# A four-layer Fourier tower in one launch: image pairs 0 and 31 stay in SBUF from layer to layer, two weight buffers in place of three, and seven eighths of mixing's chunk 0 loaded within the forward stage

## The chip, the cores and the metric

The kernel is one launch on one core of one Trainium2 chip. The metric is the device time of that launch in microseconds (us), the median of the runs shown. Five engines work from their own instruction streams and meet at semaphores: TensorE (PE, with its weight loads as PEld), VectorE (DVE), ScalarE (ACT), GpSimd (POOL) and SyncE (SP). SP does no arithmetic here; its queue issues the loads from DRAM and the stores of spectra. ACT's queue issues the stores of the layers' results besides its own work. SBUF is seen as 128 partitions; PSUM as eight banks of 128 x 512 float32.

## What is computed

A tower of four layers over 64 images of 64 x 64 pixels and 64 channels, followed by a head and a small transformer tail. All of it is float32. The layer loop, cut from the reference:

```python
for l in range(LAYERS):                                   # 4
    xf = jnp.fft.rfft2(h)                                 # only 32 x 16 modes are used
    of[:, :, :M1, :M2]  = einsum('bixy,ioxy->boxy', xf[:, :, :M1, :M2],  w1[l])
    of[:, :, -M1:, :M2] = einsum('bixy,ioxy->boxy', xf[:, :, -M1:, :M2], w2[l])
    sc = jnp.fft.irfft2(of)
    pw = einsum('bihw,oi->bohw', h, pw_w[l]) + pw_b[l]
    y = sc + pw
    y = (y - y.mean((0, 2, 3))) * rsqrt(y.var((0, 2, 3)) + EPS) * gamma[l] + beta[l]
    h = gelu(y)
out = gelu(h @ fc1_w + fc1_b) @ fc2_w + fc2_b
```

The mean and the variance go over all images, so `gelu(y)` of a layer can't be applied before the last image's `y` is there. That puts a barrier at the end of each layer.

## The kernel before, in words

The 64 images are 32 pairs (`NP`); a pair fills 128 partitions (two images x 64 channels) with 4,096 values each (`PX`), 2 MiB (2.10 MB). A layer is three stages, with all engines meeting after each (`phase_end`, L165 to L173):

- **Mixing** (`*_mix`): eight chunks (`NCH`) of the spectrum. A chunk needs its spectra of all images (`spec_in[c]`, 2 MiB, L382), its weights (`w_modes[l, c]`, 2 MiB, L375), a negated copy of the imaginary half by ACT (L460) and a copy of the real half by DVE (L471). PE multiplies (L444), DVE turns the result (L482), SP stores it in four pieces (`spec_out`, L391, 4 x 512 KiB). Three buffers for the weights, three for the spectra. After chunk c is multiplied SP loads spectra and weights of chunk c + 3, then waits for the turned result and stores it. At the end it loads the first input pair (L531) and the first group of mixed spectra (L517) ahead.
- **Inverse** (`*_inverse`): for each pair PE does the inverse transform (L581, L604) and the pointwise product with the pair's input (L595); ACT adds the bias and copies PSUM to SBUF (`y_out`, L661, four pieces T = 0 to 3), and stores the pair with two DMAs (L667); DVE turns (L697) and takes moments (L705). From layer 1 on the input pair is the stored `y` of the layer before: SP loads it (L531, three buffers `hin`), ACT applies norm and GELU in place (L653, two halves). `yout` has two buffers, so ACT's copy of pair p waits until pair p - 2 is stored. After the last pair ACT waits for both stores' semaphores, then computes the square root (L682) between DVE's L740 and L742.
- **Forward** (`*_forward`, after layers 0 to 2): SP loads `y` again (L773, four buffers `hf`, two pairs already at the end of the inverse stage, L563), ACT applies GELU (L843), DVE turns (L848, L853, L862), PE transforms (L805, L822), SP stores the spectrum of each group of four pairs (L778). The weights of the next layer's chunks 0 to 2 are loaded near its end; after the last group's store has landed, mixing begins.

Layer 0 takes the image `x` with three channels as input, so its mixing is fed by a spectrum computed at the start, and its inverse stage has no GELU. After layer 3 the head reads `y` once more (L905). The order within an engine is the order in which the code is written; nothing is rescheduled. SP's waits hold everything behind them on its queue.

Of the kernel before, what the change touches and what calls it, by code (L numbers as in the profile page):

```python
# [13 lines left out]
P = 128  # L14
C = 64
S = 64
PX = S * S
# [85 lines left out]
def build(nc, d, B, out):  # L103
# [5 lines left out]
    with ExitStack() as ctx:  # L109
# [246 lines left out]
        w_loaded = [sem(f"w_loaded{u}") for u in range(3)]  # L356
# [7 lines left out]
        w_sb = [at(u * MC * C, MC, C) for u in range(3)]  # L364
        s_sb = [at(3 * MC * C + 2 * u * B * MC, 2, B, MC) for u in range(3)]
        m_sb = [at(3 * MC * C + 6 * B * MC + 2 * u * B * HB, NG, 2, GI * HB) for u in range(2)]
        ROW = (slice(0, C), slice(C, P))
        USES = [len(range(u, NCH, 3)) for u in range(3)]

        def third(l, c):  # L370

            return l * (USES[c % 3] * 16) + (c // 3 * 16 + 16)

        def load_weights(sp, l, c):
            sp.dma_start(w_sb[c % 3], d["w_modes"][l, c]).then_inc(w_loaded[c % 3], 16)  # L375

        def sync_mix(sp, l, first):
            def load(c):
# [3 lines left out]
                sp.dma_start(s_sb[u][:, 0], spec_in[c]).then_inc(s_loaded[u], 16)  # L382
                if c > 2 or first and c == 2:
                    load_weights(sp, l, c)
# [40 lines left out]
        def tensor_mix(pe, l, first):  # L425
            for c in range(NCH):
                u, n = c % 3, l * NCH + c
                pe.wait_ge(w_loaded[u], third(l, c))
                pe.wait_ge(real_down, n + 1)
                for v in range(2):  # L430
# [3 lines left out]
                    for turn in range(4):  # L434
# [4 lines left out]
                        for k in range(4):  # L439
                            for half in range(2):  # L440
                                for row in range(2):
# [3 lines left out]
                                                   w_sb[u][ROW[row], mode, :], s_sb[u][ROW[row], :, :, mode],  # L445
# [6 lines left out]
        def scalar_mix(act, l, first):  # L452
# [3 lines left out]
            for c in range(NCH):  # L456
                u = c % 3
                act.wait_ge(s_loaded[u], third(l, c))
                for v in range(2):
                    act.activation(s_sb[u][0:C, 1, :, v * K1:(v + 1) * K1], s_sb[u][C:P, 0, :, v * K1:(v + 1) * K1],  # L460
                                   ACT.Copy, scale=-1.0).then_inc(imag_up, 1)

        def vector_mix(dve, l, first):
# [3 lines left out]
            def rotate(c):  # L467
                u = c % 3
                dve.wait_ge(s_loaded[u], third(l, c))
                dve.sem_inc(waited[dve.engine], 1)  # L470
                dve.tensor_copy(s_sb[u][C:P, 1], s_sb[u][0:C, 0]).then_inc(real_down, 1)  # L471
# [30 lines left out]
        grp = [at(off, M2, GI, HB) for off in (8 * PX, PX)]  # L502
        yout = [at((3 + u) * PX, PX) for u in range(2)]
# [3 lines left out]
        IN_USES = [len(range(b, NP, 3)) for b in range(3)]  # L507
# [25 lines left out]
        def sync_inverse(sp, l, first):  # L533
            if first:
# [3 lines left out]
                for b in range(3):  # L538
                    sp.sem_inc(in_loaded[b], IN_USES[b] * 16)
# [11 lines left out]
            for p in range(NP):  # L551
                if first:
                    load_x(p)
                elif p > 0:
# [7 lines left out]
            for q in range(2):  # L562
# [1529 lines left out]
```

## Time and profile before

| | |
|---|---|
| median of 3 runs | 4284.08 us (4277.56 to 4299.02) |
| profiled execution | 4291.21 us, its span 4289.4 us |
| PE / DVE / ACT busy | 75% / 56% / 49% of the span |
| DMA moved | 1119.64 MB, 261 GB/s over the span |
| mixing / inverse / forward of one layer (layer 1; forward ahead of it) | 137 / 418 / 287 us |
| head and tail, after the tower | about 1080 us |

The time of a stage is read from the timeline: forward 623 to 910 us, mixing 917 to 1047 us with its last store landing until 1060, inverse 1060 to 1465, then normalization until 1488. The layer pattern repeats with little change. Rows with "SPq" or "ACTq" are DMA issues on those queues; "landing" is from an issue to the completion of its bytes; what stands in brackets after a timeline row is the idle time of the engine ahead of it and who ended it.

### The profile page before, as it was taken

The page shows a single profiled execution, that of the slowest core. Times are in us where ns is not written, and L with a number is a line of the kernel's source. Part 1 is how long each engine was busy: PE and PEld are TensorE (multiplying, and loading weights), DVE is VectorE, ACT ScalarE, POOL GpSimd, SP SyncE. Part 2 cuts the span into 40 slices and gives each one's busy share as a digit, 9 for nine tenths or more (in the row PEclk, how much of TensorE's full clock was granted, in tenths as well). Part 3 has the DMA queues.
Part 4 walks back from the last instruction along what each step waited for, and adds up shares of the span by engine and source line. Part 5 has one row for each costly group of instructions (what it writes and reads, how often), then busy time and mean ns, then how long its engine had stood idle before and what let it go on. Part 6 is the DMA issues. An engine that isn't in the chain of part 4 may idle for free. (4 is left out here: it accounts for less than half of the span.)

```text
span 4289.4 us, 122178 instructions
## 1 busy us (share of the span) xinstructions
PE 3236.5 (75%) x54724; PEld 2080.3 (48%) x54724; DVE 2394.2 (56%) x3232; ACT 2090.2 (49%) x1756; POOL 28.9 (1%) x48
## 2 busy tenths in 40 slices
PE   5968866667888566687876666878869996759777
PEld 4746644456555344575554444755542221743532
DVE  3456669963666589645655996456540001454556
ACT  2123345521666555216765553166659996222322
POOL 0000000000000000000000000000000001000000
PEclk8989988888999889899998898999989998669688
DMA  8979887879999877799998786999985441012053
GB/s 314 349 196 248 226 266 276 300 287 356 364 383 374 307 284 297 272 354 364 391 379 310 290 310 269 357 358 385 387 318 207 179 165 66 1 28 53 1 106 64
DMA packets 181647, 1119.64 MB, mean 261 GB/s; under 512 B 25561, under 2 KB 31905, under 8 KB 107326
## 3 DMA queue, kind: packets, MB, share of 16 engines
q1 hardware_dynamic: 140988, 843.27, 54.3%
q10 hardware_dynamic: 39234, 269.45, 18.1%
q8 instruction: 316, 5.18, 0.5%
q0 software_dynamic: 1024, 1.05, 0.1%
q14 instruction: 85, 0.70, 0.0%
HBM read 708.56 MB, written 405.14 MB: 260 GB/s over the span
## 5 line engine op out<-in xcount | busy, mean ns | idle before, releaser
L604 PEld LDWEIGHTS bank<-fb,arena 64*64 64x64 f32 x16384 | 670.0, 199 | 521.8 <-issue 507.7
L604 PE MATMUL bank<-fb,arena 64*64 64x128 f32 x16384 | 675.4, 294 | 244.8 <-ACT arena L661 196.2
L661 ACT ACTIVATE arena<-bank,pwb 128x1024 f32<-128x1024 f32 x512 | 559.1, 1111 | 475.7 <-PE bank L595 351.3
L705 DVE BATCH_NORM_STATS2 stats<-arena 128x6 f32<-128x512 f32 x1024 | 629.0, 676 | 191.1 <-ACT arena L661 190.8
L595 PE MATMUL bank<-arena,wst 64*64 64x512 f32 x4096 | 625.6, 635 | 12.9 <-issue 12.8
L843 ACT ACTIVATE arena<-arena,shift,scale 128x1024 f32<-128x1024 f32 x384 | 443.7, 1229 | 324.9 <-DMA arena<-y_dram 324.7
L697 DVE STREAM_TRANSPOSE arena<-bank 128x512 f32<-128x512 f32 x512 | 321.1, 684 | 454.2 <-PE bank L581 454.2
L653 ACT ACTIVATE arena<-arena,shift,scale 128x2048 f32<-128x2048 f32 x192 | 401.5, 2093 | 320.0 <-issue 206.1
L805 PE MATMUL bank<-arena,fwq 32*32 32x512 f32 x6144 | 285.2, 746 | 333.6 <-DVE arena L848 333.6
L444 PE MATMUL bank<-arena 64*64 64x128 f32 x8192 | 453.9, 393 | 103.4 <-DVE arena L471 83.6
L444 PEld LDWEIGHTS bank<-arena 64*64 64x64 f32 x8192 | 397.5, 154 | 159.5 <-issue 112.2
L848 DVE STREAM_TRANSPOSE arena<-arena 128x1024 f32<-128x1024 f32 x384 | 440.0, 1203 | 16.4 <-ACT arena L843 16.4
L581 PE MATMUL bank<-arena,ga 64*64 64x512 f32 x2048 | 301.8, 613 | 90.2 <-DMA arena<-spec_out 72.6
L822 PE MATMUL bank<-arena,ghq 32*32 32x256 f32 x12288 | 351.4, 425 | 12.1 <-issue 7.6
L460 ACT ACTIVATE arena<-arena 64x2048 f32<-64x2048 f32 x64 | 118.8, 1903 | 432.9 <-DMA arena<-spec_in 432.9
L822 PEld LDWEIGHTS bank<-arena,ghq 32*32 32x32 f32 x12288 | 281.5, 111 | 86.3 <-issue 53.3
L805 PEld LDWEIGHTS bank<-arena,fwq 32*32 32x32 f32 x6144 | 96.2, 112 | 440.9 <-issue 429.1
L482 DVE STREAM_TRANSPOSE arena<-bank 128x512 f32<-128x512 f32 x256 | 159.7, 683 | 247.3 <-PE bank L444 131.3
L919 PE MATMUL bank<-arena,fc 64*128 64x512 f32 x1024 | 264.1, 624 | 18.8 <-ACT arena L947 17.4
L954 ACT ACTIVATE arena<-bank,fc1b 128x1024 f32<-128x1024 f32 x256 | 267.7, 1123 | 13.5 <-PE bank L919 13.5
L853 DVE STREAM_TRANSPOSE arena<-bank 128x1024 f32<-128x1024 f32 x192 | 226.7, 1218 | 21.2 <-PE bank L805 20.5
L972 DVE TENSOR_SCALAR arena<-bank,fc2b 128x512 f32<-128x512 f32 x8 | 6.0, 751 | 398.0 <-PE bank L930 398.0
(195 smaller groups left out, 2475.9 us busy)
## 6 DMA issues: line engine op xcount, KB each, us to landing
arena<-y_dram SPq DMA_DIRECT2D x224, 2048.0 KB, 10.3
y_dram<-arena ACTq DMA_DIRECT2D x256, 1024.0 KB, 13.4
arena<-in_w_modes SPq DMA_DIRECT2D x32, 2048.0 KB, 17.5
arena<-spec_in SPq DMA_DIRECT2D x32, 2048.0 KB, 14.6
spec_out<-arena SPq DMA_DIRECT2D x128, 512.0 KB, 14.8
arena<-spec_out SPq DMA_DIRECT2D x116, 512.0 KB, 16.5
spec_in<-arena SPq DMA_DIRECT2D x24, 2048.0 KB, 13.6
spec_in<-arena SPq DMA_DIRECT2D x4, 4096.0 KB, 12.0
```

Of the source, the lines that this page charges most:

```text
L444: mm = pe.matmul(bank[4 * v + q][ROW[half], k * 2 * B:(k + 1) * 2 * B], w_sb[u][ROW[row], mode, :], s_sb[u][ROW[row], :, :, mode], start=( ...
L581: mm = pe.matmul(bank[2 * v + r][CHAN[par], :], ga[k_p, r * S:(r + 1) * S], grp[p // Q % 2][k_p, :, par * Q + q, :], start=True, stop=True ...
L595: mm = pe.matmul(bank[4 + T % 2 * 2 + i][CHAN[v], :], wst[CHAN[i], :], hin[p % 3][CHAN[i], px:px + BK], start=False, stop=True, tile_posit ...
L604: mm = pe.matmul(hpx(bank[4 + T % 2 * 2 + i][CHAN[v], :])[:, :, j * S:(j + 1) * S], a2[p % 2][CHAN[i], v, :, 4 * T + j], hpx(fb2[CHAN[i], :]),
L653: act.activation(x, x, ACT.Gelu, bias=shift[:], scale=scale[:]).then_inc(h_ready, 1)
L661: act.activation(hpx(yout[u])[:, :, T * BK:(T + 1) * BK], banks[:, 4 + T % 2 * 2:6 + T % 2 * 2, :], ACT.Identity, bias=pwb[:]).then_inc(y_ ...
L697: dve.transpose(a2[p % 2][:, :, v * HB + c0:v * HB + c0 + 16, :].rearrange("p v c r -> p c v r"), banks[:, 2 * v:2 * v + 2, :].rearrange(" ...
L705: dve.bn_stats(stats[:, p * 48 + 6 * t:p * 48 + 6 * t + 6], hpx(yout[p % 2])[:, i, T * BK:(T + 1) * BK]).then_inc(y_seen, 1)
L805: mm = pe.matmul(bank[g][QUAD[c], :], fwq[QUAD[g], s * 32:(s + 1) * 32], hT[q % 2][QUAD[g], s, :, c * CQ:(c + 1) * CQ], start=(s == 0), st ...
L822: mm = pe.matmul(bank[4 + c][QUAD[j], 0:256], ghq[QUAD[c], col:col + K1], t1[q % 2][QUAD[c], v:4:2, hh, :, ri * M2:(ri + 1) * M2], start=( ...
L843: act.activation(x, x, ACT.Gelu, bias=shift[:], scale=scale[:]).then_inc(f_ready, 1)
L848: dve.transpose(hT[p % 2][:, :, 16 * v:16 * v + 16, :].rearrange("p s h c -> p h s c"), hf[p % Q][:, v * 2 * BK:(v + 1) * 2 * BK].rearrang ...
```

## The change

Two pieces of 4,096 values per partition at the top of the arena, `kept[0]` and `kept[31]`, hold pairs 0 and 31 from the inverse stage of one layer to that of the next. For them `y_out` writes straight into `kept` (it was one activation of 128 x 1024 a piece, and is four of 64 x 512, since the layout that the store's DMA used to make is now made by the copy), nothing is stored, the forward stage and the head apply GELU in place and don't load, and the next inverse stage finds them with GELU already applied, so it neither loads them nor applies it. `FED` is the list of the other 30 pairs; counts of semaphores follow it.

The room comes from mixing: two weight buffers (`NW = 2`), and five pieces for the spectra where there were six: real halves in three, second planes in two (`planes`), so that ACT's and DVE's plane copies of chunk c wait for chunk c - 2's product. With two buffers the weights of chunk c + 2 are loaded after the product of chunk c, ahead of the spectra of chunk c + 3; only chunks 0 and 1 are loaded within the forward stage. In the freed place there the spectra of images 0 to 55 of chunk 0 are loaded too, after the stores of the groups 0 to 6; the last eight images follow at mixing's start.

```diff
+        NW = 2
+        KEPT = (0, 31,)
+        kept = {p: at(ARENA - (i + 1) * PX, PX) for i, p in enumerate(KEPT)}
+        FED = [p for p in range(NP) if p not in KEPT]
...
-        w_sb = [at(u * MC * C, MC, C) for u in range(3)]
-        s_sb = [at(3 * MC * C + 2 * u * B * MC, 2, B, MC) for u in range(3)]
+        w_sb = [at(u * MC * C, MC, C) for u in range(NW)]
+        s_all = at(NW * MC * C, 5, B, MC)
...
+        EARLY = B - GI
+        def load_spectra(sp, c, images):
+            sp.dma_start(s_all[:, c % 3, images], spec_in[c][:, images]).then_inc(s_loaded[c % 3], 16)
+        def planes(c):
+            first, second = c % 3, 3 + c % 2
+            return s_all[:, first:second + 1:second - first]
...
             for c in range(NCH):
+                if NW == 2 and c + 2 < NCH:
+                    sp.wait_ge(mix_done, (l * NCH + c) * 2 + 2)
+                    load_weights(sp, l, c + 2)
                 if c + 3 < NCH:
                     load(c + 3)
                 store(c)
                 if c == NCH - 3:
-                    if not first:
+                    if not first and 0 not in KEPT:
                         load_input(sp, l, 0)
...
                 act.wait_ge(s_loaded[c % 3], spectra_count(l, c))
+                if c > 1:
+                    act.wait_ge(mix_done, (l * NCH + c) * 2 - 2)
...
+                if p in KEPT:
+                    act.wait_ge(y_done, n * 4 + (T + 9))
+                    act.sem_inc(waited[act.engine], 1)
+                    for i in range(2):
+                        for v in range(2):
+                            px = v * HPX + T * BK
+                            k = act.activation(kept[p][CHAN[i], px:px + BK], bank[4 + T % 2 * 2 + i][CHAN[v], :], ACT.Identity,
+                                               bias=pwb[CHAN[v], :])
+                    k.then_inc(y_copied, 1)
+                    return
...
             store(lf * NG + (NG - 2), NG - 2)
-            for c in range(3):
+            for c in range(NW):
                 sp.wait_ge(px_turned, (lf * NP + NP + c) * 4 + 4)
                 load_weights(sp, lf + 1, c)
+            sp.wait_ge(px_turned, (lf * NP + NP + NW) * 4 + 4)
+            sp.wait_ge(spec_stored[0], lf * (NG // 2 * 16) + (NG // 2 * 16 + 16))
+            sp.wait_ge(spec_stored[1], lf * (NG // 2 * 16) + NG // 2 * 16)
+            load_spectra(sp, 0, slice(0, EARLY))
             store(lf * NG + (NG - 1), NG - 1)
```

SP from the end of the forward stage into mixing, before (L375 is a load of weights, L778 the store of a group's spectrum, L382 a load of spectra, L172 the meeting of the engines):

```order
L375 DMA arena<-in_w_modes 128x4096
L777 ISA
L778 DMA spec_in<-arena 128x8x512 [waits hdft_turned]
L793 ISA
L172 ISA [waits spec_stored_even,spec_stored_odd]
L382 DMA arena<-spec_in 128x4096 [waits phase_done]
L382 DMA arena<-spec_in 128x4096 x2
```

The same place after the change (L392 weights, L376 spectra, L828 the store):

```order
L392 DMA arena<-in_w_modes 128x4096
L841 ISA
L843 ISA [waits px_turned]
L845 REGISTER_ALU [waits spec_stored_even]
L376 DMA arena<-spec_in 128x3584 [waits spec_stored_odd]
L827 ISA
L828 DMA spec_in<-arena 128x8x512 [waits hdft_turned]
L172 ISA [waits spec_stored_even,spec_stored_odd]
L376 DMA arena<-spec_in 128x512 [waits phase_done]
L376 DMA arena<-spec_in 128x4096 x2
```

The third load of weights has gone from here, 3,584 of chunk 0's 4,096 values have come ahead of the last store, and 512 are left behind the meeting.

SP within mixing, one chunk, before (L391 stores the mixed chunk):

```order
L381 ISA
L382 DMA arena<-spec_in 128x4096 [waits mix_done]
L375 ISA
L375 DMA arena<-in_w_modes 128x4096
L387 ISA
L391 DMA spec_out<-arena 32x4096 [waits mixed_turned]
L391 DMA spec_out<-arena 32x4096 x3
```

and after:

```order
L432 ISA
L392 ISA [waits mix_done]
L392 DMA arena<-in_w_modes 128x4096
L398 ISA
L376 DMA arena<-spec_in 128x4096 [waits mix_done]
L409 ISA
L413 DMA spec_out<-arena 32x4096 [waits mixed_turned]
L413 DMA spec_out<-arena 32x4096 x3
```

The weights now go ahead of the spectra, and they are those of the chunk after the next one.

ACT at the end of an inverse stage (pair 31, then the square root), before:

```order
L653 ACTIVATE arena<-arena,shift,scale 128x2x1024
L659 ISA [waits y_stored_odd]
L660 ISA [waits y_seen]
L661 ACTIVATE arena<-bank,pwb 128x2x512 [waits y_done]
...
L664 REGISTER_ALU
L667 DMA y_dram<-arena 64x2x2048 [waits y_copied]
L667 DMA y_dram<-arena 64x2x2048
L678 REGISTER_ALU
L680 ISA [waits y_stored_odd,y_stored_even]
L682 ACT_TABLE_LOAD [waits bn_step]
L682 ACTIVATE bn<-bn 128x1
```

and after (L703 copies pair 31):

```order
L717 DMA y_dram<-arena 64x2x2048
L698 ISA
L703 ACTIVATE arena<-bank,pwb 64x512 [waits y_done]
L703 ACTIVATE arena<-bank,pwb 64x512 x3
...
L728 ISA
L730 ISA [waits y_stored_odd,y_stored_even]
L732 ACT_TABLE_LOAD [waits bn_step]
L732 ACTIVATE bn<-bn 128x1
```

Pair 31's GELU, its wait for a free buffer and its two stores are gone; the wait for stored pairs stays, and the last of them is pair 30.

## Rows read from the trace of the kernel before

**Rows 1.** Busy time by stretch, layer 0's forward to layer 1's end; columns in its first line.
```profile
core 0: us, PE busy (x) PEld busy (x) DVE busy (x) ACT busy (x) POOL busy (x), PEclk, DMA share, GB/s
622.00:910.00 288.00, 185.93 (x6144) 125.59 (x6144) 259.48 (x257) 149.23 (x129) 0.00 (x0) 0.88 0.77 292
910.00:1047.00 137.00, 113.33 (x2048) 98.46 (x2048) 56.41 (x70) 29.70 (x16) 0.00 (x0) 0.90 0.91 349
...
1064.00:1100.00 36.00, 28.96 (x468) 17.47 (x470) 19.71 (x33) 18.49 (x15) 0.00 (x0) 0.88 0.85 321
1100.00:1350.00 250.00, 202.58 (x3524) 134.38 (x3526) 151.97 (x243) 166.94 (x121) 0.00 (x0) 0.92 1.00 385
1350.00:1450.00 100.00, 81.97 (x1448) 55.08 (x1452) 60.49 (x97) 67.97 (x50) 0.00 (x0) 0.92 0.94 342
```

**Rows 2.** Who waited for whom, whole span: total us, times, longest us.
```profile
DVE bn L742 <- ACT bn L682: 44.0, 4, 12.3
```

**Rows 3.** DVE's timeline around the square root, layers 0, 1, 2 and 3.
```profile
611.58 0.15 DVE L740 TENSOR_SCALAR bn<-bn 128x1 f32<-128x1 f32 x1
621.30 0.17 DVE L742 RECIPROCAL bn<-bn 128x1 f32<-128x1 f32 x1 [9.57 <-ACT bn L682]
...
1482.98 0.16 DVE L742 RECIPROCAL bn<-bn 128x1 f32<-128x1 f32 x1 [12.29 <-ACT bn L682]
...
2347.16 0.16 DVE L742 RECIPROCAL bn<-bn 128x1 f32<-128x1 f32 x1 [9.96 <-ACT bn L682]
...
3207.43 0.16 DVE L742 RECIPROCAL bn<-bn 128x1 f32<-128x1 f32 x1 [12.20 <-ACT bn L682]
```

**Rows 4.** ACT's timeline at layer 3's end: pair 30's stores, the square root's table.
```profile
3179.29 1.24 ACTq L667 DMA_DIRECT2D y_dram<-arena  x2
...
3205.90 1.28 ACT L682 ACT_TABLE_LOAD   x1 [17.05 <-DMA y_dram<-arena]
```

**Rows 5.** Landing times of DMAs on y_dram issued at 3179.2 to 3181, pair 30's among them.
```profile
DMA to landing us min/median/max: 15.4/20.4/20.7
```

**Rows 6.** Groups by line, whole span: busy us, mean ns | idle us ahead and its releaser.
```profile
L661 ACT ACTIVATE arena<-bank,pwb 128x1024 f32<-128x1024 f32 x512 | 559.1, 1111 | 475.7 <-PE bank L595 351.3 <-DMA y_dram<-arena 114.2 <-issue 4.2
L653 ACT ACTIVATE arena<-arena,shift,scale 128x2048 f32<-128x2048 f32 x192 | 401.5, 2093 | 320.0 <-issue 206.1 <-POOLq L171 113.9
L1288 ACT ACTIVATE arena<-bank 64x512 f32<-64x512 f32 x16 | 9.5, 594 | 32.2 <-PE bank L1221 32.0
```

**Rows 7.** ACT's timeline in layer 1's inverse stage: pair 0's store, pair 2's first copy.
```profile
1082.92 1.25 ACTq L667 DMA_DIRECT2D y_dram<-arena  x2
...
1098.63 2.12 ACT L661 ACTIVATE arena<-bank,pwb 128x1024 f32<-128x1024 f32 x2 [1.14 <-DMA y_dram<-arena]
```

**Rows 8.** SP's timeline in layer 1's mixing: chunks 0 to 2's spectra, chunk 3's.
```profile
917.15 1.28 SPq L382 DMA_DIRECT2D arena<-spec_in  x3
...
942.12 0.32 SPq L382 DMA_DIRECT2D arena<-spec_in  x1
```

**Rows 9.** ACT's timeline there: spectra of chunks 0, 3, 5 and 7 arriving.
```profile
924.88 3.71 ACT L460 ACTIVATE arena<-arena 64x2048 f32<-64x2048 f32 x2 [45.19 <-DMA arena<-spec_in]
...
950.29 3.72 ACT L460 ACTIVATE arena<-arena 64x2048 f32<-64x2048 f32 x2 [10.82 <-DMA arena<-spec_in]
...
989.60 3.71 ACT L460 ACTIVATE arena<-arena 64x2048 f32<-64x2048 f32 x2 [16.36 <-DMA arena<-spec_in]
...
1019.24 3.71 ACT L460 ACTIVATE arena<-arena 64x2048 f32<-64x2048 f32 x2 [11.14 <-DMA arena<-spec_in]
```

**Rows 10.** Landing of the weights issued at 1003.3 in that mixing stage.
```profile
DMA to landing us min/median/max: 21.1/21.1/21.1
```

**Rows 11.** PE and DVE at that stage's end: one chunk's product, the last turn.
```profile
1032.06 14.20 PE L444 MATMUL bank<-arena 64*64 64x128 f32 x256 [0.95 <-DVE arena L482]
...
1046.34 2.51 DVE L482 STREAM_TRANSPOSE arena<-bank 128x512 f32<-128x512 f32 x4 [4.50 <-PE bank L444]
```

**Rows 12.** DMA issues by line: count, KB each, median us to landing.
```profile
arena<-comb SPq DMA_DIRECT2D x32, 256.0 KB, 5.4
```

More of the change, by code:

```diff
@@ L381, in load @@
                     sp.wait_ge(mix_done, (l * NCH + c) * 2 - 4)
-                sp.dma_start(s_sb[u][:, 0], spec_in[c]).then_inc(s_loaded[u], 16)
-                if c > 2 or first and c == 2:
+                if c > 0:
+                    load_spectra(sp, c, slice(0, B))
+                else:
+                    if first:
+                        load_spectra(sp, c, slice(0, EARLY))
+                    load_spectra(sp, c, slice(EARLY, B))
+                if NW == 3 and (c > 2 or first and c == 2):
                     load_weights(sp, l, c)
@@ L426, in tensor_mix @@
             for c in range(NCH):
-                u, n = c % 3, l * NCH + c
-                pe.wait_ge(w_loaded[u], third(l, c))
+                u, n, s_c = c % NW, l * NCH + c, planes(c)
+                pe.wait_ge(w_loaded[u], uses(l, c, NW))
                 pe.wait_ge(real_down, n + 1)
@@ L467, in rotate @@
             def rotate(c):
-                u = c % 3
-                dve.wait_ge(s_loaded[u], third(l, c))
+                s_c = planes(c)
+                dve.wait_ge(s_loaded[c % 3], spectra_count(l, c))
+                if c > 1:
+                    dve.wait_ge(mix_done, (l * NCH + c) * 2 - 2)
                 dve.sem_inc(waited[dve.engine], 1)
-                dve.tensor_copy(s_sb[u][C:P, 1], s_sb[u][0:C, 0]).then_inc(real_down, 1)
+                dve.tensor_copy(s_c[C:P, 1], s_c[0:C, 0]).then_inc(real_down, 1)
             rotate(0)
@@ L501, in build @@
         hin = [at(off, PX) for off in (2 * PX, 7 * PX, 0)]
-        grp = [at(off, M2, GI, HB) for off in (8 * PX, PX)]
-        yout = [at((3 + u) * PX, PX) for u in range(2)]
+        grp = [at(off, M2, GI, HB) for off in (4 * PX, PX)]
+        yout = [at(off, PX) for off in (3 * PX, 8 * PX)]
         a2 = [at(5 * PX + u * PX // 2, 2, C, M1) for u in range(2)]
@@ L506, in build, with fed @@
         HPX = PX // 2
-        IN_USES = [len(range(b, NP, 3)) for b in range(3)]
+        IN_FED = [[p for p in FED if p % 3 == b] for b in range(3)]
+        Y_FED = [[p for p in FED if p % 2 == u] for u in range(2)]
+        F_FED = [[p for p in FED if p % Q == q] for q in range(Q)]
+        def fed(lists, l, p):
+            mine = lists[p % len(lists)]
+            return l * (len(mine) * 16) + (len([r for r in mine if r < p]) * 16 + 16)
         CHAN = (slice(0, C), slice(C, P))
@@ L553, in sync_inverse @@
                     load_x(p)
-                elif p > 0:
+                elif p > 0 and p not in KEPT:
                     load_input(sp, l, p)
@@ L561, in sync_inverse @@
             sp.sem_inc(waited[sp.engine], 1)
-            for q in range(2):
-                sp.dma_start(hf[q], y_dram[q]).then_inc(f_loaded[q], 16)
+            for p in FED[:2]:
+                sp.dma_start(hf[p % Q], y_dram[p]).then_inc(f_loaded[p % Q], 16)
         def tensor_inverse(pe, l, first):
@@ L590, in pointwise @@
             def pointwise(p, T):
+                h = hin[p % 3] if first or p not in KEPT else kept[p]
                 for i in range(2):
```

62 lines of the change are left out of this document (36 added, 26 removed).

## The prediction, made before the changed kernel was run

> **What bounds the kernel now.** I read the busy time by stretch first [rows 1], then who waits for whom [rows 2], then the timelines at the three seams of a layer [rows 3, 4, 7, 8, 9, 11]. One layer shows three limits. The forward stage is DVE's: 259 of 288 us busy, with DMA at 0.77. The middle of the inverse stage is the DMA engines': share 1.00 and 385 GB/s from 1100 to 1350, while PE is busy 203 of 250 us. Mixing is PE's and nearly DMA's: 113 of 137 us, DMA 0.91; a chunk's product is 14.2 us [rows 11]. Between them lie seams in which nothing computes: at each layer's end DVE stands 9.57 to 12.29 us before L742, 44.0 us in all four [rows 2, 3], because ACT waits for the last pair's store before the square root [rows 4]; at mixing's start ACT and DVE wait from SP's issue at 917.15 to 924.88, 7.7 us, for chunk 0 [rows 8, 9].
>
> **The end of a layer.** Pair 31 is no longer stored. Once DVE is ready there remain the table load and the root, 3207.43 - 3205.90 = 1.5 us [rows 3, 4]: 44.0 - 4 x 1.5 = 38 us at most. Two deductions. The four copies of 64 x 512 cost 4 x 0.594 = 2.4 us a piece against 1.11 [rows 6], 1.3 us more; pair 31's last piece is on the path. In layers 1 to 3 ACT loses pair 31's two halves of GELU (2 x 2.09) and the issue of its stores (1.2), which covers the 5.1 us of the four pieces. Layer 0 has no GELU, so there I take 2.3 us off (one to two pieces). Second, pair 30's store is now the last to wait for. In layer 3 it is issued at 3179.3 to 3179.9 and lands up to 20.7 us later [rows 4, 5], about 3200.6, and DVE is ready at 3207.4 - 12.2 = 3195.2. But pair 31's 2.10 MB shared the DMA engines; at 385 GB/s they are 5.4 us, so pair 30 may land up to that much sooner. Bounds: 5.3 us saved in each layer (21 in all) if it lands as late as there, 38 - 2 = 36 if it is never late. I take 1 us lateness a layer on average, nearer to the upper end since layer 3 is an extreme of the four: **32 us saved**.
>
> **The inverse stage, layers 1 to 3.** Of its DMA work pair 0's store and pair 31's load go, 2.10 MB each, 5.4 us at 385 GB/s. But neither lies in the saturated middle: the share is 0.85 around pair 0 and 0.94 after 1350 [rows 1]. For pair 0 ACT's row of work becomes longer: four pieces at 2.4 and two halves of GELU for pair 1, 13.7 us against 8.6. Counting on from the first piece at about 1075.5, pair 1's store is issued some 2.8 us later than before; pair 2's first copy, which waited until 1098.63 for pair 0's store [rows 7], comes at the same time, with an emptier DMA queue behind it. So I take 1.5 us gained at the start (0 to 5.4), 1.5 for pair 31's load (0 to 5.4) and 1 for its GELU while ACT is the late one: 4 us, times three, **12 us saved**; bounds 0 and 33. In layer 0 neither load nor GELU exists; 0.
>
> **Mixing's start, layers 1 to 3.** Left behind the meeting of the engines is 256 KiB instead of 2 MiB. The nearest row with that size lands in 5.4 us [rows 12]; taking the bytes alone off (1.84 MB at 385 GB/s, 4.8 us) would leave 2.9 of the 7.7. I take 4.1, between them, so 3.6 us a layer: **11 us saved**, bounds 7 and 14. In layer 0 both pieces are loaded at the same moment: 0. The part moved into the forward stage takes the place of the third weights on SP's queue and waits for the group 6 store; behind it in that queue is only the last store, over 10 us away, and PE's and DVE's work there doesn't depend on it: 0. Were it late, at most its own 4.8 us would show. The loads dropped in the forward stage and the head gain nothing, since DVE bounds the one and no wait for DMA ends last in the other.
>
> **Within mixing.** Here is what the change pays. Weights of chunk c + 2 are asked for when product c ends and must be there when product c + 1 ends, 14 us on. Before, there were two such spans. Spectra issued at 942.12 arrive at 950.29; those of chunk 5 and 7, one and then two steps later in a row that never empties, at 989.60 and 1019.24 [rows 8, 9]. SP's queue moves 2.10 MB transfers in order: from 950.29 to 989.60 six of them, 6.6 us each; from 989.60 to 1019.24 six, 4.9 us each. Now the weights are the first of each three. With t = 0 at the end of product 0 they are transfers 1, 4, 7, 10, 13, 16. Reading the old arrivals as the times of transfers 1, 7 and 13 (8, 47 and 77 us after 942.12; 4 and 10 between them) and adding three of 4.9, chunk 7's weights land at 92, its product ends at 106. Before, the last turn begins at 1046.34, so that product ended at 104. Cost 2 us a layer; with a uniform (1019.24 - 942.12 - 2) / 13 = 5.8 us a transfer 4 to 5 us. At the end input 0 isn't loaded, so the transfers between t = 0 and the last store are as many as before in layers 1 to 3. I take 1.5 us there and 2 in layer 0: **7 us lost**; bounds 24 won (PE never waits: 7 x 14.2 = 99 for 104) and 68 lost (rival d). The added waits of ACT and DVE for product c - 2 hold nothing: that product is over a full 14 us before the planes are needed, ACT's two copies are 3.7 us [rows 9], and DVE had to wait for it anyway to turn it.
>
> The Trainium skill, "DMA: Bandwidth & Descriptors", section on bandwidth, gives about 358 GB/s as one core's share of HBM. The 250 us at 385 GB/s [rows 1] are above it, so by the row it isn't a ceiling here. By the page a transfer would be 5.9 us; what that makes of mixing is the second rival.
>
> **Sum.** 32 + 12 + 11 - 7 = 48 us. Against the profiled execution's 4291.2 that is 4243; the median of the runs is 7.1 us lower, so **4236 us**, 1.1% faster.
>
> **Rivals.**
> (a) The saturated inverse stage gives back all bytes: 33 us instead of 12, 4215 us. For it speaks the share of 1.00 for 250 us; against it, that both transfers lie outside. Chance 0.13.
> (b) Mixing's transfers take 5.9 us from start to end, so weights 7 land at 2 + 16 x 5.9 = 96 and product 7 ends at 110, 6 us later than now. That is 24 us instead of 7, 4253 us. For it speaks the mean of 5.8. Chance 0.12. The page's figure, given above, would lead to the same.
> (c) The wait only moves: pair 30's store lands as late as the rows say (21 for 32) and pair 0's longer copies eat the inverse gain (0 for 12). 48 - 23 = 25, 4259 us. Chance 0.11.
> (d) Transfers run at 6.6 us throughout: product 7 ends at 2 + 106 + 14 = 122, 17 us late, 68 us in four layers for 7; 4297 us, no change. For it speaks the first half of the old row; against it the second half. Chance 0.14.
> (e) Slower: the weights are not helped by going first, and land as one did before, 21.1 us after issue [rows 10], 7 us after they are needed. Six such in a layer are 42 us, four layers 168, for the 7: 4397 us. It decides from the point where the six are late by more than 55 / 24 = 2.3 us each, that is when they land over 16.3 us after issue. Against it: in the old order spectra stood ahead of them, and a late product also delays the requests behind, so that the queue drains. Chance 0.08.
>
> **How the numbers follow.** Forecast 0.42, its own range 4225 to 4250. Above (c) lie 0.14 and 0.08, of which the range takes in the part of (d) in which only some transfers are slow; below, it takes in (a) with the upper bounds of the seams: 4208 to 4275. About 0.5% (21 us) is what a measurement of this kernel can tell from no change. Faster than that, below 4263: forecast, (a), (b) and (c), 0.78. Same: (d), 0.14. Slower: 0.08.
>
> **What would show it.** DVE's idle time before the reciprocal: 1.5 to 4 us a layer instead of 9.6 to 12.3; if 5 or more, pair 30 is late, (c). From SP's first issue in mixing to ACT's first plane copy: near 4 us. PE's waits for weights within mixing: under 4 us a layer; over 12, (d); over 14 with landings above 16.3, (e). DMA share at the start of layer 1's inverse lower than 0.85 and the stretch from pair 0 to pair 31 shorter by about 4 us; by 10, (a). The forward stages unchanged at 287 us; if they grow, the early spectra disturb DVE's loads, which I have priced at nothing, and the forecast is wrong there.

## The result and the profile after

Median of 20 runs 4279.82 us (4245.75 to 4295.97), beside 4294.09 us of the kernel before (20 runs, 4271.38 to 4306.87): ratio 0.996 [0.9944, 0.9977]. That is some 17 us faster. The prediction was 4236 us and 48 us faster; its range ended at 4275. The profiled execution took 4269.44 us (before: 4291.21). Its page begins and ends so:

```profile
span 4267.4 us, 122303 instructions
...
DMA packets 177905, 1073.52 MB, mean 252 GB/s; under 512 B 25145, under 2 KB 31489, under 8 KB 107422
...
arena<-in_w_modes SPq DMA_DIRECT2D x32, 2048.0 KB, 15.1
spec_out<-arena SPq DMA_DIRECT2D x128, 512.0 KB, 15.0
arena<-spec_out SPq DMA_DIRECT2D x116, 512.0 KB, 16.1
arena<-spec_in SPq DMA_DIRECT2D x28, 2048.0 KB, 18.3
```

The bytes are gone as meant: 1119.64 MB before. The last column is the landing time. Who waited for whom, whole span, in the kernel after (L792 is the old L742, L732 the old L682, L469 the product, L703 the new copies of pairs 0 and 31, L756 DVE's moments):

```profile
PE bank L469 <- DMA arena<-in_w_modes: 11.9, 8, 3.3
DVE bn L792 <- ACT bn L732: 7.7, 4, 2.7
ACT arena L487 <- PE bank L469: 53.4, 6, 10.3
DVE stats L756 <- ACT arena L703: 50.4, 24, 6.2
PE bank L641 <- ACT arena L703: 22.0, 22, 2.2
DVE stats L756 <- ACT arena L711: 153.9, 132, 3.0
PE bank L641 <- ACT arena L711: 174.4, 95, 4.5
```

and in the kernel before (L661 copies all pairs):

```profile
PE bank L604 <- ACT arena L661: 196.2, 97, 6.2
DVE stats L705 <- ACT arena L661: 190.8, 148, 3.4
```

The second row answers [rows 2]: 44.0 us became 7.7, the gain that the change was to bring. The first is new: before, PE never waited for weights. DVE's waits for copies grew from 190.8 to 204.3 us, which is about what the end of the layers will be found to have lost below. PE's are 196.4 us for 196.2: they moved to the pairs that stay, but their sum did not grow. The stretches of [rows 1] (PE's first work in the inverse stage is at 1063.58 us here, and was at 1064.44):

```profile
core 0: us, PE busy (x) PEld busy (x) DVE busy (x) ACT busy (x) POOL busy (x), PEclk, DMA share, GB/s
620.00:908.00 288.00, 187.48 (x6091) 126.36 (x6098) 258.35 (x256) 149.01 (x129) 0.00 (x0) 0.86 0.74 276
908.00:1045.00 137.00, 115.72 (x2114) 106.41 (x2105) 57.26 (x70) 29.70 (x16) 0.00 (x0) 0.89 0.89 336
1064.00:1100.00 36.00, 28.62 (x455) 16.64 (x451) 17.29 (x28) 22.72 (x24) 0.00 (x0) 0.90 0.63 238
1100.00:1350.00 250.00, 205.16 (x3573) 137.23 (x3569) 155.88 (x249) 170.10 (x124) 0.00 (x0) 0.92 1.00 384
1350.00:1450.00 100.00, 84.38 (x1521) 57.93 (x1517) 63.65 (x102) 67.93 (x50) 0.00 (x0) 0.95 0.95 338
```

In the first 36 us of the inverse stage the DMA engines moved 238 GB/s where they moved 321: 3.0 MB less, of which pair 0's store explains 2.1. ACT was busy for 22.7 us instead of 18.5, PE and DVE a little less than before. So the queue was emptied and not refilled.

**Sums by stage.** The timelines give the starts and ends of each step. I added them over the four layers for each profiled kernel. "First" is the time to the first product of mixing (from the last group's store; in layer 0 from the launch), "mixing" goes from there to the end of the last turn, "run-up" from PE's first work in the inverse stage to the issue of pair 30's store, "tail" from there to the last moments' sum, "root" from there to the reciprocal, and "forward" from the first GELU to the last group's store.

| kernel | first | mixing | run-up | tail | root | forward |
|---|---|---|---|---|---|---|
| before | 145.5 | 483.9 | 1525.5 | 49.6 | 63.4 | 862.4 |
| after | 134.8 | 495.1 | 1527.6 | 62.0 | 27.2 | 861.8 |
| after, second profile (`changed_again`) | 132.8 | 500.1 | 1525.2 | 63.0 | 28.5 | 862.4 |
| as predicted | -11 | +7 | -12 | +2 | -34 | 0 |
| `both_one_copy` | 134.8 | 496.8 | 1502.7 | 54.3 | 29.0 | 862.1 |
| `both_split` | 135.3 | 494.3 | 1512.9 | 59.1 | 31.9 | 871.7 |
| `both_no_early` | 147.2 | 492.1 | 1541.9 | 66.2 | 27.0 | 858.3 |
| `both_spectra_first` | 132.5 | 510.4 | 1548.0 | 60.2 | 28.9 | 864.2 |
| `k31_w3_early` | 133.6 | 478.8 | 1521.3 | 59.8 | 27.4 | 865.1 |
| its repeat | 133.5 | 481.6 | 1526.1 | 59.4 | 27.0 | 868.3 |
| `k31_w3` | 146.9 | 486.6 | 1525.6 | 64.7 | 27.1 | 863.5 |
| `k31_w2_early` | 133.7 | 496.3 | 1524.7 | 68.3 | 26.2 | 858.7 |
| `k31_w3_early_split` | 134.3 | 480.6 | 1529.4 | 55.3 | 29.2 | 863.7 |
| `w2_only` | 147.1 | 492.4 | 1524.6 | 49.0 | 63.2 | 864.8 |
| `no_store0` | 145.4 | 481.3 | 1527.0 | 50.5 | 61.3 | 863.9 |

Each row is one execution. The code of the forward stage's work is nearly the same in all, yet its column goes from 858 to 872, and run-ups of kernels with the same inverse stage (after, `both_no_early`, `both_spectra_first`) from 1525 to 1548. The tails of the eight profiles with the same code there (all but the first row, `both_one_copy`, the two split kernels and the last two rows) go from 59.4 to 68.3. So from one profile I read no difference under 15 us in the forward, 23 in the run-up and 9 in the tail; the other columns repeat within some 5. After minus before is -10.7, +11.2, +2.1, +12.4, -36.2, -0.6, together -22, as the two spans differ; what is left out changes by under 1 us between these two. Between others it changes more: from the last reciprocal to the end (head and transformer tail, where the kernels hardly differ) it is 1082.0 us before, 1080.5 to 1083.8 in the kernels with pairs 0 and 31, 1084.3 in `k31_w2_early`, but 1075.9 to 1077.3 in the four profiles of pair 31 with three buffers, in `w2_only` and in `no_store0`. Why is open. First, root and forward came out as predicted or better. Tail and run-up did not.

### The profile page after: what moved, and what is told of

Its sections match the earlier page's. It is cut to its first block and busy times, and to the rows that moved or that the text cites. A ratio compares the mean times of both kernels' runs of the same rounds, so it can differ in the third digit from the quotient of the medians.

```text
span 4267.4 us, 122303 instructions
## 1 busy us (share of the span) xinstructions
PE 3245.1 (76%) x54724; PEld 2074.8 (49%) x54724; DVE 2397.3 (56%) x3232; ACT 2118.4 (50%) x1840; POOL 29.0 (1%) x48
## 3 DMA queue, kind: packets, MB, share of 16 engines
q0 software_dynamic: 1024, 1.05, 0.1%
## 5 line engine op out<-in xcount | busy, mean ns | idle before, releaser
L756 DVE BATCH_NORM_STATS2 stats<-arena 128x6 f32<-128x512 f32 x1024 | 630.3, 677 | 205.2 <-ACT arena L711 153.9
L711 ACT ACTIVATE arena<-bank,pwb 128x1024 f32<-128x1024 f32 x480 | 523.7, 1112 | 350.2 <-PE bank L632 235.8
L632 PE MATMUL bank<-arena,wst 64*64 64x512 f32 x4096 | 626.9, 630 | 15.1 <-issue 15.1
L469 PE MATMUL bank<-arena 64*64 64x128 f32 x8192 | 457.8, 393 | 98.0 <-DVE arena L500 71.0
L693 ACT ACTIVATE arena<-arena,shift,scale 128x2048 f32<-128x2048 f32 x180 | 376.7, 2093 | 197.9 <-issue 197.7
L469 PEld LDWEIGHTS bank<-arena 64*64 64x64 f32 x8192 | 396.5, 155 | 159.1 <-issue 110.2
## 6 DMA issues: line engine op xcount, KB each, us to landing
arena<-in_w_modes SPq DMA_DIRECT2D x32, 2048.0 KB, 15.1
arena<-spec_in SPq DMA_DIRECT2D x28, 2048.0 KB, 18.3
```

The source lines that it names most:

```text
L469: mm = pe.matmul(bank[4 * v + q][ROW[half], k * 2 * B:(k + 1) * 2 * B], w_sb[u][ROW[row], mode, :], s_c[ROW[row], :, :, mode], start=(swap ...
L632: mm = pe.matmul(bank[4 + T % 2 * 2 + i][CHAN[v], :], wst[CHAN[i], :], h[CHAN[i], px:px + BK], start=False, stop=True, tile_position=(i * ...
L693: act.activation(x, x, ACT.Gelu, bias=shift[:], scale=scale[:]).then_inc(h_ready, 1)
L711: act.activation(hpx(yout[u])[:, :, T * BK:(T + 1) * BK], banks[:, 4 + T % 2 * 2:6 + T % 2 * 2, :], ACT.Identity, bias=pwb[:]).then_inc(y_ ...
L756: dve.bn_stats(stats[:, p * 48 + 6 * t:p * 48 + 6 * t + 6], y[:, i, T * BK:(T + 1) * BK]).then_inc(y_seen, 1)
```

## Where the copies cost

ACT's timeline at the start of layer 1's inverse stage, kernel after (start, length, in brackets idle time ahead of it and its cause):

```profile
1074.74 5.57 ACT L703 ACTIVATE arena<-bank,pwb 64x512 f32<-64x512 f32 x8 [51.30 <-PE bank L632]
1080.33 2.10 ACT L693 ACTIVATE arena<-arena,shift,scale 128x2048 f32<-128x2048 f32 x1
1082.46 5.56 ACT L703 ACTIVATE arena<-bank,pwb 64x512 f32<-64x512 f32 x8
...
1097.43 1.26 ACTq L717 DMA_DIRECT2D y_dram<-arena  x2
```

Eight copies take 5.57 us, one every 0.697. A piece is 2.79 us, not the 2.4 of the forecast, which had taken the price from L1288 [rows 6]. That copy has no bias from a tile. The Trainium skill ("ScalarE: Activation LUTs", section "What ACT_TABLE_LOAD costs") says that each operand read by a pointer adds about 93 ns. By the profile one copy of L703 lasts 683 ns at the mean and one of L1288 594, a difference of 89 ns, in agreement; 14 ns more pass until the next one starts. PE stands behind ACT here, kernel after:

```profile
1080.45 1.21 PE L641 MATMUL bank<-fb,arena 64*64 64x128 f32 x32 [0.73 <-ACT arena L703]
...
1085.37 1.22 PE L641 MATMUL bank<-fb,arena 64*64 64x128 f32 x32 [1.99 <-ACT arena L703]
```

From the first copy to the end of pair 0's last it is 13.3 us (1074.74 to 1088.02). In the kernel before it was 7.3:

```profile
1075.51 1.11 ACT L661 ACTIVATE arena<-bank,pwb 128x1024 f32<-128x1024 f32 x1 [11.01 <-PE bank L595]
...
1081.69 1.11 ACT L661 ACTIVATE arena<-bank,pwb 128x1024 f32<-128x1024 f32 x1 [0.31 <-PE bank L595]
...
1092.62 2.73 ACTq L667 DMA_DIRECT2D y_dram<-arena  x2
...
1107.85 1.25 ACTq L667 DMA_DIRECT2D y_dram<-arena  x2
```

Pair 1's store is issued 33.9 us after PE's first work of the stage (1063.58), before 28.2 (1064.44): 5.7 us later, not 2.8. Pair 2's follows in the kernel after at

```profile
1107.12 2.77 ACTq L717 DMA_DIRECT2D y_dram<-arena  x2
```

That is 43.5 us after the first work, and 43.4 in the kernel before (1107.85). Before, pair 2's copies had waited for pair 0's store; that wait is gone, and what it gave is used up by the 5.7 us. From there on the changed kernel is behind: pair 3's store leaves after 57.1, 57.4 and 55.8 us in layers 1 to 3 (55.6, 57.2 and 57.0 in its second profile), before after 53.1, 53.3 and 53.7. By pair 30 the difference is -3.6, +1.0 and +6.2 us, and -1.6 in layer 0 (second profile -4.3, -2.8, +0.8 and +6.0): the saturated stretch varies by more than the start has cost.

The end of the stage, ACT and then DVE in the kernel after:

```profile
1449.03 1.26 ACTq L717 DMA_DIRECT2D y_dram<-arena  x2
1450.58 11.15 ACT L703 ACTIVATE arena<-bank,pwb 64x512 f32<-64x512 f32 x16 [1.67 <-issue]
...
1453.38 1.29 DVE L756 BATCH_NORM_STATS2 stats<-arena 128x6 f32<-128x512 f32 x2 [2.62 <-ACT arena L703]
1456.18 1.28 DVE L756 BATCH_NORM_STATS2 stats<-arena 128x6 f32<-128x512 f32 x2 [1.51 <-ACT arena L703]
```

and ACT in the kernel before:

```profile
1454.78 2.10 ACT L653 ACTIVATE arena<-arena,shift,scale 128x2048 f32<-128x2048 f32 x1 [1.41 <-issue]
1456.78 2.10 ACT L661 ACTIVATE arena<-bank,pwb 128x1024 f32<-128x1024 f32 x2
1460.15 1.11 ACT L661 ACTIVATE arena<-bank,pwb 128x1024 f32<-128x1024 f32 x1 [1.27 <-PE bank L595]
1463.21 1.11 ACT L661 ACTIVATE arena<-bank,pwb 128x1024 f32<-128x1024 f32 x1 [1.95 <-PE bank L595]
```

After the change sixteen copies stand in one row without a gap and DVE waits for each four of them. Before, ACT waited for PE twice in pair 31, 3.2 us in all. Set the two stretches side by side from pair 30's store on. The copies of pair 31 take 11.15 us of ACT where they took 4.3, which is 6.8 more. Of the 5.4 us that the forecast set against them only one half of GELU, 2.1 us, lies here: the other half ran before pair 30's store, and the issue of pair 31's stores (1.2) came behind its last copy, where the moments no longer depend on it. The 3.2 us of waiting took up another part. That leaves 1.5 us; the stretch grew from 12.2 to 14.0 us, by 1.9. In layer 2 it grew by 1.5. In layer 3 ACT stood 5.3 us for PE before pair 31's first copy and it grew by 6.8, in layer 0 by 2.3. In the second profile it is 3.1, 2.4, 4.1 and 3.9 us, layers 0 to 3.

## The experiments

Theory: the four copies a piece are what the forecast lost (the tail, pair 0's delay). Rivals: the two weight buffers cost more than 7 us; the bytes of pairs 0 and 31 were worth nothing; the early spectra disturb the forward stage. Ratios are against runs of the kernel before on the same chip. The edits shown are the part that matters; where buffers change their places with them, that is left out. Three batches: the kernel before 4295.19, 4294.72 and 4296.09 us there.

**One copy a piece.** Pairs 0 and 31 keep the layout of a stored pair; the later stages read them as if it were their own, so these pairs' values are permuted.

```diff
-for i in range(2):
-    for v in range(2):
-        px = v * HPX + T * BK
-        k = act.activation(kept[p][CHAN[i], px:px + BK], bank[4 + T % 2 * 2 + i][CHAN[v], :], ACT.Identity, bias=pwb[CHAN[v], :])
+k = act.activation(hpx(kept[p])[:, :, T * BK:(T + 1) * BK], banks[:, 4 + T % 2 * 2:6 + T % 2 * 2, :], ACT.Identity, bias=pwb[:])
```

> The changed kernel with each kept piece copied by one activation of 128 x 1024, as stored pairs are, instead of four of 64 x 512; the two middle quarters of a kept pair lie exchanged by it, so later layers compute on other data of the same size. It prices the four copies alone. Theory 1 (the copies use up what pair 0's missing store gives): pair 1's store 27 to 29 us after the stage's first product instead of 33 to 34, pair 30's some 3 us earlier, the end of the layer 2 us shorter: 20 to 25 us less than the changed kernel, 4256. Theory 2 (the stages vary by chance and the copies are hidden): within 8 us of 4280.

4246.92 us (6 runs), ratio 0.9889 [0.9856, 0.9923], against 0.996 and, measured again, 0.9948 [0.9925, 0.9971] of the changed kernel. That is 25 to 30 us less by the two ratios, a little more than was expected, and 48 us less than before, the sum of the forecast. The table puts it in the run-up (-23 against before) and the tail (+5 for +12). Both come from one profile, and both lie below the four profiles that keep pairs 0 and 31 with four copies (run-up 1525 to 1548, tail 60 to 66); how the 25 to 30 us divide between the two is not shown more finely. The same 36 us at the stage's start, kernel `both_one_copy`, whose stage begins 7.8 us earlier:

```profile
1056.00:1092.00 36.00, 32.61 (x544) 20.35 (x546) 21.00 (x35) 21.39 (x16) 0.00 (x0) 0.85 0.78 299
```

and ACT there:

```profile
1067.64 1.12 ACT L700 ACTIVATE arena<-bank,pwb 128x1024 f32<-128x1024 f32 x1 [52.24 <-PE bank L632]
...
1083.83 1.27 ACTq L714 DMA_DIRECT2D y_dram<-arena  x2
...
1093.56 2.73 ACTq L714 DMA_DIRECT2D y_dram<-arena  x2
```

Pair 1's store leaves 28.0 us after the first work (1055.81), as before the change, and pair 2's 37.8, 5.7 us sooner than in the kernel before or the changed one. Pair 3's leaves after 52.4, 50.2 and 51.4 us in layers 1 to 3, 3 to 8 us sooner than in the four profiles just named. The DMA engines move 299 GB/s where the changed kernel has 238, 2.2 MB or 5.7 us at 385 GB/s more. This is the largest missed term, shown by its removal.

**Half of the copies to DVE.**

```diff
+def copy_half(p, T):
+    dve.wait_ge(y_done, (l * NP + p) * 4 + (T + 9))
+    for v in range(2):
+        px = v * HPX + T * BK
+        k = dve.tensor_scalar(kept[p][CHAN[1], px:px + BK], bank[5 + T % 2 * 2][CHAN[v], :], pwb[CHAN[v], :], None, ALU.add)
+    k.then_inc(y_half, 1)
```

> The changed kernel, but of the four copies of a kept piece ACT makes two and DVE the other two, side by side. Theory 1: a kept piece takes 1.4 us instead of 2.8, pair 1's store comes 29 to 30 us after the first product instead of 33 to 34, pair 31 ends 2 to 4 us earlier; 15 to 20 us less than the changed kernel in four layers, 4260 to 4265. Theory 2: the same as the changed kernel, 4280.

4272.17 us, 0.9947 [0.9924, 0.997]. In layers 1 to 3 pair 1's store leaves at 28.8 to 29.9 us, so the delay at the start is cured. The tail is 3 us shorter, within its spread. Yet against the changed kernel (0.996, 0.9948) the time is hardly different, a miss. Root is 5 us longer: in layers 1 and 3 ACT's table load waits for pair 30's store, which lands about 21 us after its issue, so DVE stands 4.4 and 4.7 us before the reciprocal where the changed kernel had 2.7 and 1.6. Ending the moments sooner gains nothing beyond that point. The rest of the missing gain stays open. With pair 31 alone:

> Only pair 31 kept, three weight buffers, early spectra, and pair 31's pieces copied half by ACT and half by DVE. Theory 1: against the same kernel without the shared copies, 4246.5, pair 31's end is 1 to 3 us a layer shorter, 4238 to 4243. Theory 2: DVE's copies come between its moments and give it back: 4247.

4252.3 us, 0.9902 [0.9872, 0.9931], the same as without it (below). The tail is 4 to 5 us shorter, all four layers together, and below the eight profiles with four copies by ACT. Root takes back 2 of it, for the same reason (4.4 us before the reciprocal in layer 3), and the run-up is not shorter. The expectation was missed: in the time of the runs the rest does not show.

**Two weight buffers alone**, no pair kept, nothing early:

```diff
-        KEPT = (0, 31,)
+        KEPT = ()
```

> No pair is kept and all spectra are loaded at mixing's start; only the weight buffers are two, with the changed kernel's order of loads, and input 0 lies elsewhere. Theory 1: mixing is 3 to 4 us a layer longer than before's 121, 11 to 17 us in all, 4306 to 4312. Theory 2 (two buffers cost nothing, the changed kernel's mixing is longer by the moved spectra): 4295, mixing stages as before.

4302.51 us, 1.0021 [1.0002, 1.0041]: 9 us slower, a little less than was expected. Mixing is 8.5 us longer, the only column that changes by over 3. The forecast's 7 for this was right. (The head of this profile is 5.4 us shorter than before's, which is not in the table.)

**Without the early spectra:**

```diff
-            load_spectra(sp, 0, slice(0, EARLY))
```

At mixing's start chunk 0 is loaded whole, as before.

> The changed kernel without the early spectra: chunk 0 is loaded whole at mixing's start. It prices the early load alone. From the last group's store to the first product 17.7 us instead of 13.5, three times: 12 to 13 us more than the changed kernel, 4292. If the early load also costs the forward stage something, or saves DMA work within mixing, it is less or more than that; mixing and forward stages show which.

4287.11 us, 0.9986 [0.9963, 1.001]: 11 to 16 us slower than the changed kernel by its two ratios. The first product comes 12 to 14 us later as predicted, but mixing is 3 to 8 us shorter, which takes part of it back.

**Pair 31 alone**, with three weight buffers (the place of pair 0 holds the third) and the early spectra, then without them, then with two buffers:

```diff
-        NW = 2
-        KEPT = (0, 31,)
+        NW = 3
+        KEPT = (31,)
```

> Only pair 31 is kept; pair 0 is stored and loaded as before, three weight buffers stay, and seven eighths of chunk 0's spectra are still loaded in the forward stage. Theory 1 (the changed kernel's inverse stages were longer because each piece of a kept pair costs 2.8 us of ACT, four copies of 0.70, and pair 0 at the start holds PE up; two weight buffers cost the mixing stage 11 us): against before's 4294 the seam before the reciprocal gives 36, mixing's start 12, pair 31's copies take back 8: about 4254. Pair 1's store comes 28 to 29 us after the stage's first product, as before. Theory 2 (the inverse stage is longer by something else, such as where its buffers lie or how its DMAs queue): 4265 to 4275, inverse stages still at 403 us on average.

> Only pair 31 kept, three weight buffers, chunk 0's spectra all loaded at mixing's start as before. It measures the end of the layer alone. Theory 1: DVE's wait before the reciprocal falls from 44 us to under 10, pair 31's copies take 8 back, so 28 us less than before, 4266. Theory 2: under 20 us less. From the last group's store to the first product of mixing 17.7 us, as before.

> Only pair 31 kept, two weight buffers, early spectra; input 0 is loaded ahead into the place that pair 0 had. Against the first of these kernels it changes the weight buffers alone, against the changed kernel pair 0 alone. Theory 1: mixing 2 to 4 us a layer longer than with three buffers, 11 us in all, 4265; start of the inverse stages as before. Theory 2: mixing's extra time was chance, and it comes out within 4 us of the first kernel.

`k31_w3_early` 4246.51 us (6 runs), 0.9904 [0.9873, 0.9935]; `k31_w3` 4267.88, 0.9943 [0.9917, 0.9968]; `k31_w2_early` 4274.46, 0.996 [0.994, 0.9979]. The first was some 8 us better than expected, the last 9 us worse. Keeping pair 31 alone is worth 24 to 27 us, less than the 36 in "root", since the tail grows by 10 to 19. Its load, 2.1 MB a layer, does not show: in the five profiles with pair 31 alone the run-up is 1521 to 1529, 1525.4 at the mean, against 1525.5 and 1524.6 without it. The early spectra are worth 15 to 21 us here and 7 to 16 with pair 0 and two buffers. With the early load the third buffer is worth 28 us by the medians, 24 by the ratios; `w2_only`, without it, puts it at 9. The profiles put only 15 to 18 us of it in mixing. 8.5 to 8.9 are in the tail and 8.0 to 8.4 in the head, whose code is the same in both kernels; why they differ is open.

ACT's plane copies in layer 1's mixing show where. `k31_w3_early`:

```profile
906.92 3.71 ACT L487 ACTIVATE arena<-arena 64x2048 f32<-64x2048 f32 x2 [46.31 <-DMA arena<-spec_in]
...
952.11 3.71 ACT L487 ACTIVATE arena<-arena 64x2048 f32<-64x2048 f32 x2 [10.25 <-PE bank L469]
970.06 3.71 ACT L487 ACTIVATE arena<-arena 64x2048 f32<-64x2048 f32 x2 [14.24 <-DMA arena<-spec_in]
...
999.37 3.72 ACT L487 ACTIVATE arena<-arena 64x2048 f32<-64x2048 f32 x2 [10.95 <-DMA arena<-spec_in]
```

and the changed kernel:

```profile
921.52 3.71 ACT L487 ACTIVATE arena<-arena 64x2048 f32<-64x2048 f32 x2 [48.04 <-DMA arena<-spec_in]
...
971.92 3.73 ACT L487 ACTIVATE arena<-arena 64x2048 f32<-64x2048 f32 x2 [15.40 <-DMA arena<-spec_in]
988.55 3.72 ACT L487 ACTIVATE arena<-arena 64x2048 f32<-64x2048 f32 x2 [12.91 <-DMA arena<-spec_in]
...
1019.73 3.71 ACT L487 ACTIVATE arena<-arena 64x2048 f32<-64x2048 f32 x2 [10.95 <-DMA arena<-spec_in]
```

From chunk 0's copy to chunk 7's it is 92.5 us with three buffers and 98.2 with two, where it was 94.4 before [rows 9].

**Only pair 0's store removed** from the kernel before; its readers take pair 1:

```diff
-            sp.dma_start(hin[p % 3], y_dram[p]).then_inc(in_loaded[p % 3], 16)
+            sp.dma_start(hin[p % 3], y_dram[max(p, 1)]).then_inc(in_loaded[p % 3], 16)
...
+                        if p == 0:
+                            act.sem_inc(y_stored[u], 16)
+                            continue
```

> The kernel before, with pair 0 not stored in the inverse stages; whoever read it reads pair 1 (so pair 0's later layers are computed on pair 1's data). Nothing else changes: it measures what 2.1 MB less to store at the start of a DMA-full stage is worth. Theory 1 (the bytes are worth 3 to 5 us a layer, and the changed kernel spends them on pair 0's copies): pair 30's store 3 to 5 us earlier in the stages of layers 1 to 3, 12 to 18 us less in all, 4278 to 4283. Theory 2 (the stage's pace is set by the ring of loads and stores, not by their sum, so a missing store at its edge gives nothing): 4290 to 4295, pair 30's store as before.

4285.71 us, 0.9974 [0.9955, 0.9994]: 10 us, about 2.6 a layer, half of the 5.4 us of the transfer, and a little less than expected. At the start of the stage the gain can be seen: pair 3's store leaves after 50.3, 50.3 and 51.6 us in layers 1 to 3, 2 to 3 us sooner than in the kernel before. The run-up (+1.5) doesn't show it, and pair 30's store is not 3 to 5 us earlier, as was expected, but from 8.8 earlier to 7.2 later. Of the 7.6 us by which this profile's span is shorter 5.3 lie in the head. So the bytes count at the start, above the 1.5 taken; whether the 10 us are theirs alone isn't shown.

**Spectra asked for ahead of the weights**, the order of before:

```diff
+                if c + 3 < NCH:
+                    load(c + 3)
                 if NW == 2 and c + 2 < NCH:
                     sp.wait_ge(mix_done, (l * NCH + c) * 2 + 2)
                     load_weights(sp, l, c + 2)
-                if c + 3 < NCH:
-                    load(c + 3)
```

> The changed kernel, with the spectra of chunk c + 3 asked for ahead of the weights of chunk c + 2 on SP's queue, as the old order had it. Theory 1 (transfers are served in order, and with two buffers the weights are on the path): each chunk's weights come one transfer, 5 to 6 us, later; from chunk 4 or 5 on PE waits that much more, mixing is 4 to 7 us a layer longer, 16 to 28 us in all over the changed kernel. Theory 2 (weights are early enough, mixing is longer for another reason): as the changed kernel.

4298.37 us, 0.9997 [0.9978, 1.0016], 21 us (ratios) to 26 us (medians) above the changed kernel on the same chip, as expected. Landing times and PE's wait in this kernel, against 15.1, 18.3 and 11.9 above:

```profile
PE bank L469 <- DMA arena<-in_w_modes: 28.0, 13, 5.8
...
arena<-in_w_modes SPq DMA_DIRECT2D x32, 2048.0 KB, 16.3
...
arena<-spec_in SPq DMA_DIRECT2D x28, 2048.0 KB, 12.6
```

The weights land only 1.2 us later at the median, but they are what PE needs next: mixing is 10 to 15 us longer. The rest stands in the run-up (1548), and isn't explained.

**Repeats** of the changed kernel and of the best one:

> The changed kernel once more, for a second profile of its stages: inverse stages 1580 to 1600 us in sum with pair 1's store 33 to 34 us after the first product and pair 30's at 385 to 391; mixing stages 494 to 497. 4275 to 4285.

> The kernel that keeps pair 31 alone with three weight buffers and early spectra, once more, beside the changed kernel on the same chip. Expected 4245 to 4255, 25 to 35 us below the changed kernel. If it were chance the first time, within 15 us of it.

4272.13 us, 0.9948 [0.9925, 0.9971], and 4252.48 us (6 runs), 0.99 [0.9875, 0.9925]. The changed kernel came out 3 us below what was expected, with a mixing of 500.1 for 494 to 497; `k31_w3_early` lies 20 us below it, where 25 to 35 were expected. So the changed kernel is 0.4 to 0.5% faster than before, and the version with pair 31 alone and three buffers 1.0%, better than both kernels.

## Why the prediction was wrong, point by point

**The end of the layer: right.** DVE's idle time before the reciprocal, changed kernel:

```profile
619.54 0.16 DVE L792 RECIPROCAL bn<-bn 128x1 f32<-128x1 f32 x1 [1.72 <-ACT bn L732]
...
1470.77 0.16 DVE L792 RECIPROCAL bn<-bn 128x1 f32<-128x1 f32 x1 [2.67 <-ACT bn L732]
...
2326.33 0.16 DVE L792 RECIPROCAL bn<-bn 128x1 f32<-128x1 f32 x1 [1.63 <-ACT bn L732]
```

These are the 1.5 to 4 us named. "Root" fell by 36.2 us where 34 were taken, so the 4 us set off for pair 30's lateness were too many. The first half of rival (c), pair 30 late, fell by this. Its second half came true: "pair 0's longer copies eat the inverse gain (0 for 12)" is what the two profiles show (+2 and 0).

**The cover of the copies: the step that failed.** "Which covers the 5.1 us of the four pieces" set all work that ACT loses with pair 31 against all that it gains, without asking which of it stands between pair 30's store and the last moments. Measured, the tail is 12.4 us longer (13.4 in the second profile) where 2 were taken. Layer 0, with 2.3 and 3.1 us for 2.3, was right or nearly so; layers 1 to 3 lost 10 us where nothing was taken. Two errors are in it. Of the 5.4 us of removed work 2.1 lie in that stretch; the first half of GELU had even been counted again, as the 1 us won in the inverse stage. And the copy comes every 0.697 us and not every 0.594: 16 x 0.103 = 1.6 us a pair, 6.6 in four layers for pair 31. That it was not worse is luck: 3.2 us of waits for PE in layer 1, which the forecast did not see either, took up part of the added work. Why ACT waited 5.3 us for PE before pair 31's first copy in layer 3 stays open.

**The inverse stage: the second step that failed, by the same copies at its other end.** 12 us were to be saved; the run-up changed by +2 and 0 in the two profiles of the changed kernel. Pair 0's bytes have a worth at the stage's start (`no_store0`, pair 3's store 2 to 3 us sooner), pair 31's load shows none, and pair 1's store, issued 5.7 us later where 2.8 were taken, leaves the DMA engines idle at the start (share 0.63 for the 0.78 with one copy). "Pair 2's first copy comes at the same time, with an emptier DMA queue behind it" held for the queue alone: the copy came 37.2 us after the stage's first work (1100.74) for 34.2 before, 3.0 later, and an emptier queue is no gain when nothing is there to fill it. With one copy a piece the run-up was 23 us shorter in its one profile (7.6, 5.7, 5.8 and 3.7 us in layers 0 to 3; layer 0 varies by 11 us between kernels that have the same code there). That lies midway between the forecast's 12 and the 33 of rival (a), all bytes back, and doesn't tell them apart.

**Mixing's start: right.** From SP's issue at 917.97 to ACT's first plane copy at 921.52 is 3.55 us ("near 4"); "first" fell by 10.7 and 12.7 us for 11.

**Within mixing: right in kind, low in size.** 11.2 us and, in the second profile, 16.2 for 7; `w2_only` 8.5. (The bound "24 won" is a slip: 104 - 99 is 5 us a layer, some 20.) PE's waits for weights are 11.9 us in four layers, 3 a layer ("under 4"), landings 15.1 at the median, under the 16.3 of rival (e). What was missed is that the early load and two buffers don't add up. Mixing without early spectra: 483.9, 486.6 and 481.3 with three buffers, 492.4 and 492.1 with two. With them: 478.8, 481.6 and 480.6 with three, 494.3 to 500.1 with two. The early load shortens mixing by some 4 us with three buffers and lengthens it by 4 with two. Each is no more than one profile's spread; with three buffers the two groups touch (481.3 and 481.6), with two they don't. A likely reason, argued only: mixing starts 4 us sooner, and with two buffers the weights are still asked for one product ahead.

**The forward stage: right**, 861.8 and 862.4 for 862.4.

**The sum.** The errors of the profiled execution are +14 (run-up), +10 (tail), +4 (mixing), -2 (root), 26 us in all; 48 - 26 = 22, the difference of the spans. The kernel with one copy a piece was faster by the 48 us of the forecast. Its terms differ from mine (run-up -23, tail +5, mixing +13) and balance by luck; what it shows is the size of the copies' part, 25 to 30 us.

## What to carry to other kernels

When work is taken from an engine and other work added to it, look in the timeline where each piece stands: removed work covers added work only between the same two events of the path, and idle time there takes up added work too. Here 2.1 of 5.4 us of removed work stood in the right place. A store or load that disappears is worth its transfer time only if the requests behind it come sooner; if the step that replaces it delays them, the DMA engines stand idle instead. Two edits on one queue (here an earlier first chunk and one buffer less) are to be measured together, since each can use up what the other leaves.

## What I had not expected of the hardware

- A copy of 64 x 512 from PSUM took 683 ns with its bias from a tile and 594 without [rows 6], and four of them 2.79 us for the 1.11 of one 128 x 1024 copy of the same values: half the partitions, 2.5 times the price.
- Changing the order of two requests on one queue, both of 2 MiB and both issued within a microsecond, was worth 21 to 26 us (0.9948 and 0.9997), of which mixing's column shows 10 to 15: spectra landed in 18.3 us behind the weights and in 12.6 ahead of them.
